# Moving the fourth group's convolution taps, y's statistics, a state carry and one factor operation in a fused Mamba and mixture-of-experts kernel

## The reference

```python
x = x + LN(mamba(LN(x)))
x = x + LN(moe(LN(x)))

# mamba, 512 inner channels, 16 states
x_in, z = split(x @ W_in)
u = silu(causal_conv(x_in, conv_w, 4 taps) + conv_b)
dt, B, C = split(u @ W_xproj)
delta = softplus(dt @ W_dt + b_dt)
h[t] = exp(delta[t] * A) * h[t-1] + delta[t] * u[t] * B[t]    # for each channel and state
y[t] = sum over the states of h[t] * C[t]
out = ((y + D_skip * u) * silu(z)) @ W_out

# moe: a shared MLP of width 256, and 8 experts of width 128, the best 2 of a softmax router
out = shared(x) + sum over e of coef[e] * (silu(x @ gate[e]) * (x @ up[e])) @ down[e]
```

## Time and profile before

| | |
|---|---|
| three runs, median (lowest to highest) | 2396.18 us (2395.93 to 2397.23) |
| the profiled execution's own time | 2396.12 us |
| its span, first to last instruction | 2394.3 us |
| mean granted TensorE clock | 0.932 |
| busy: TensorE, VectorE | 87%, 91% of the span |
| busy: ScalarE, GpSimd | 70%, 80% of the span |

### The profile page before, as it was taken

One profiled execution on the slowest core, in us unless ns is written; L12 is line 12 of the kernel. 1 busy time (PEld: TensorE's weight loads), 2 busy tenths in 40 slices (PEclk: granted clock), 3 DMA queues, 4 the chain that ended last, 5 costly groups with the idle time before them and its releaser, 6 DMA issues. The chain is left out here.

```text
span 2394.3 us, 30302 instructions
## 1 busy us (share of the span) xinstructions
PE 2081.6 (87%) x9216; PEld 1359.5 (57%) x9216; DVE 2189.5 (91%) x3112; ACT 1666.7 (70%) x2484; POOL 1908.7 (80%) x1566
## 2 busy tenths in 40 slices
PE   6668989899898989989898998989889898996977
PEld 2345565656556565665656556565655656565544
DVE  2999999999999999999999999999999999998950
ACT  4557777777877776877777687777777777775632
POOL 3576897969889797888979788797988979698844
PEclk8759999999999999999999999999999999998989
DMA  4111121111121111211111121121111211111201
GB/s 130 37 36 44 61 61 49 59 57 58 53 62 60 52 56 56 61 54 59 58 54 49 54 71 58 54 58 52 56 54 63 62 50 58 49 57 47 68 21 45
DMA packets 92946, 134.27 MB, mean 56 GB/s; under 512 B 12000, under 2 KB 42976, under 8 KB 92784
## 3 DMA queue, kind: packets, MB, share of 16 engines
q1 hardware_dynamic: 92784, 132.34, 18.3%
HBM read 123.13 MB, written 9.18 MB: 55 GB/s over the span
## 5 line engine op out<-in xcount | busy, mean ns | idle before, releaser
L793 DVE TENSOR_TENSOR_SCAN h<-d_a,carry,d_bu 128x512 f32<-128x512 f32 x1024 | 1262.1, 1267 | 53.6 <-ACT d_a L615 45.4
L1024 POOL TENSOR_TENSOR d_bu<-delta_u,b_rows 128x1024 f32<-128x1024 f32 x512 | 1202.2, 2362 | 4.9 <-DMA b_rows<-b_rows_hbm 0.8
L615 ACT ACTIVATE d_a<-delta,a_neg 128x512 f32<-128x512 f32 x1024 | 696.4, 689 | 481.7 <-DVE h L793 479.9
L449 PE MATMUL ht<-ident,h 128*128 128x128 f32 x4096 | 624.0, 299 | 148.0 <-DVE y_t L803 141.1
L449 PEld LDWEIGHTS ht<-ident,h 128*128 128x128 f32 x4096 | 515.4, 153 | 371.2 <-DVE y_t L803 142.1
L803 DVE SCALAR_TENSOR_TENSOR y_t<-ht,c_t,y_t 128x512 f32<-128x512 f32 x896 | 621.2, 735 | 2.7 <-PE ht L449 2.0
L524 PE MATMUL ring<-x_t,w_gate_sb 128*128 128x512 f32 x640 | 321.0, 627 | 23.1 <-ACT delta L758 19.0
L531 PE MATMUL ring<-x_t,w_up_sb 128*128 128x512 f32 x640 | 301.9, 616 | 22.7 <-ACT silu_gate L708 22.5
L551 PE MATMUL dn<-w_down_sb,up_hidden 128*128 128x256 f32 x1280 | 304.3, 381 | 15.8 <-POOL up_hidden L1082 15.8
L1077 POOL TENSOR_TENSOR up_hidden<-silu_gate,up_hidden 128x512 f32<-128x512 f32 x160 | 204.6, 1278 | 125.9 <-ACT up_hidden L712 77.4
L551 PEld LDWEIGHTS dn<-w_down_sb,up_hidden 128*128 128x128 f32 x1280 | 235.9, 190 | 77.4 <-issue 28.7
(11 more groups left out here) (114 smaller groups left out, 1922.0 us busy)
## 6 DMA issues: line engine op xcount, KB each, us to landing
b_rows<-b_rows_hbm SPq DMA_DIRECT2D x256, 256.0 KB, 3.5
coef_rows<-coef_rows_hbm SPq DMA_DIRECT2D x128, 256.0 KB, 3.4
xa<-L_attn_x_in SPq DMA_DIRECT2D x16, 512.0 KB, 5.0
xr<-L_attn_x_in SPq DMA_DIRECT2D x16, 512.0 KB, 5.2
out<-xr SPq DMA_DIRECT2D x16, 512.0 KB, 2.9
w_in_sb<-L_attn_W_in_in SPq DMA_DIRECT2D x1, 1024.0 KB, 6.3
w_gate_sb<-L_ffn_experts_gate_in SPq DMA_DIRECT2D x2, 512.0 KB, 4.9
w_up_sb<-L_ffn_experts_up_in SPq DMA_DIRECT2D x2, 512.0 KB, 5.6
```

The costliest lines, as they stand in the source:

```text
L449: last = nc.tensor.transpose(HT[q % HTS][:, j * P:(j + 1) * P], H[:, (NS * c + n) % HS, j, a * P:(a + 1) * P], IDN[:, :])
L615: nc.scalar.activation(DA[i % DAS][:, :], DL[:, r, j, :], ACT.Exp, scale=ANEG[:, j, n:n + 1]).then_inc(ex.sem, 1)
L793: nc.vector.tensor_tensor_scan(H[:, (NS * s + n) % HS, j, :], DA[(n * J + j) % DAS][:, :], BU[:, (2 * n + j // 2) % 4, j % 2, :], CARRY[:, ...
L1024: nc.gpsimd.tensor_tensor(BU[:, (2 * n + h) % 4, :, :], DU[:, 2 * h:2 * h + 2, :], BB[:, n % 2, :].unsqueeze(1).to_broadcast([P, 2, T]), A ...
```

## The change

Five things are moved or rewritten. The three taps of group 3 go from slot 11 to slot 12 on DVE, where they stand behind slot 12's scan and ahead of its two additions. The silu of u's groups 2 and 3 goes from slot 11 to slot 12 on ACT, and with it stands behind one more decay. y's statistics go from slot 60 to slot 61 on DVE. On POOL, the carry of state 15 goes behind the first inflow of slot 0. And y's factors take four operations in place of five: o's product is now negated when o's factors are made (four operations there in place of three), and y's last operation subtracts y's product from it.

```diff
-        shift = {w: stage(f"shift_{w}", n) for w, n in dict(xa=2, o=1, x1=2, y=3).items()}
+        shift = {w: stage(f"shift_{w}", n) for w, n in dict(xa=2, o=2, x1=2, y=2).items()}
...
-        XIN_PE, TAP0_ACT, CONV = (3, 4, 7, 8), (4, 5, 8, 8), (6, 7, 10, 11)
+        XIN_PE, TAP0_ACT, CONV = (3, 4, 7, 8), (4, 5, 8, 8), (6, 7, 10, 12)
...
-        Z_PE, Z_ACT, Y_STATS = 9, (8, 8, 9, 9), 60
+        Z_PE, Z_ACT, Y_STATS = 9, (8, 8, 9, 9), 61
         U_EARLY, HEAD_POOL = 7, 15
-        SILU = {11: [("u", 2), ("u", 3)], 60: [("z", j) for j in range(J)]}
-        SILU_FIRST = {11: SILU[11] + SILU[60]}
+        SILU = {12: [("u", 2), ("u", 3)], 60: [("z", j) for j in range(J)]}
+        SILU_FIRST = {12: SILU[12] + SILU[60]}
...
                 nc.gpsimd.tensor_tensor(MR[w][:, :], MV[w][:, :, 0], RS[w][:, :], ALU.mult)\
                   .then_inc(shift[w].sem, 1)
+                pool.wait_ge(shift[w].sem, shift[w].at(c, 1))
                 if w == "y":
-                    pool.wait_ge(shift["y"].sem, shift["y"].at(c, 1))
                     pool.wait_ge(shift["o"].sem, shift["o"].at(c))
-                    nc.gpsimd.tensor_tensor(MR["y"][:, :], MR["y"][:, :], MR["o"][:, :], ALU.add)\
+                    nc.gpsimd.tensor_tensor(MR["y"][:, :], MR["o"][:, :], MR["y"][:, :], ALU.subtract)\
                       .then_inc(shift["y"].sem, 1)
-                if w != "o":
-                    pool.wait_ge(shift[w].sem, shift[w].at(c, 2 if w == "y" else 1))
+                else:
                     nc.gpsimd.tensor_tensor(MR[w][:, :], MR[w][:, :], MINUS4[:, :], ALU.mult)\
                       .then_inc(shift[w].sem, 1)
...
                     if exists(lo - 2) and t == 0:
                         rstd_of("y", s - 2)
-                    if t == 0 and ffn:
-                        keep_state(s - 1, o, NS - 1)
...
                     if with_scan and n + 1 < NS and t % 2 == 0:
                         inflow(s, n + 1, t % NT // 2)
+                    if t == 0 and ffn:
+                        keep_state(s - 1, o, NS - 1)
```

## The result

The changed kernel takes 2381.6 us (median of 4 runs, 2381.41 to 2383.07), the kernel before 2396.05 us beside it: a ratio of 0.994, with a 95% interval from 0.9926 to 0.9953. The forecast was 2382.5 us, in a range of 2376 to 2389.

What follows compares the result with a forecast made beforehand. DVE, busy 91% of the span, was taken as the bound, with its work kept, so only its idle could go. Terms 5.6 + 5.9 + 0.4 + 0.3 + 1.4 = 13.6 us off 2396.12 gave 2382.5 us, range 2376 to 2389.

Steps and rivals of the forecast that it cites:

- Part A: Slots 11 to 14, taps and silu moved: 0.48 us gained a chunk, 1.1 lost in the first, 5.6 in all.
- the new wait of scan 12: Slot 11: without taps there, scan 12 waits 0.43 us for decay 12, against 0.91 gained at scan 14.
- ACT's room behind decay 16: ACT, slots 12 to 17: decay 16 can start at 1214.2, ACT is free at 1214.0, only 0.2 us of room.
- The slower rival: Slots 12 to 17: ACT's round ends too late if loads cost twice 1.28 us; 33 us lost, 2416; chance 0.03.
- Parts B and C: Chunk boundary: y's statistics moved and POOL's edits together gain 0.42 us at 14 boundaries, 5.9; neither does much alone.
- B: Slot 61: y's statistics no longer wait; scan 62 comes 0.50 us earlier, with 0.45 left at scan 63.
- The clock: TensorE's slow clock at chunk changes: 0.1 us a chunk credited, 1.4 in all; bounds 7.7 less, 5.4 more.
- the three lengths of before: Steady chunks of 140.54, 141.48 and 141.26 us, read as three reaches of TensorE's slow clock, 140.54 being clean.
- The ends: Last chunk ends 0.4 us earlier; one operation less in y's last factors behind it saves 0.3.
- Part C: POOL, into slot 4: scan 4 may start 0.43 us earlier, 0.28 for the operation and 0.15 for the carry.

Runs made afterwards that it cites:

- a_only: Kernel before, with only the taps of group 3 and the silu of u's last groups moved to slot 12; 2389.97 us, ratio 0.9972.
- silu_only: Kernel before, with the silu of u's last groups moved to slot 12 and the taps left in slot 11; 2404.63 us, ratio 1.0032.
- taps_only: Kernel before, with the taps of group 3 moved to slot 12 and the silu left in slot 11; 2398.35 us, ratio 1.0007.
- c_only: Kernel before, with only the carry put behind the inflow and four operations for y's factors on POOL; 2396.54 us, ratio 0.9999.
- warm: The change plus four matmuls a chunk, whose result nobody reads, on TensorE in slot 60; 2381.76 us, ratio 0.9932 to the kernel before.
- b_only: Kernel before, with only y's statistics moved to slot 61; 2389.78 us, ratio 0.9972.
- a_and_b: The change without the carry's move and with five operations for y's factors; 2383.04 us, ratio 0.9944 to the kernel before.
- decay_12_13: The change, with decay 12 ahead of z's last two copies and decay 13 ahead of x1's transposed copies on ACT; 2380.14 us, ratio 0.9931.
- pad_small: The change plus one idle DVE reduction of 128 x 192 values a chunk in slot 24; 2382.26 us, ratio 0.9937 to the kernel before.
- warm_12_13: decay_12_13 plus the four unread matmuls a chunk on TensorE in slot 60; 2379.71 us, ratio 0.9926 to the kernel before.

## Why the prediction was right

- **Part A**, forecast 14 x 0.48 - 1.1 = 5.6. Measured 0.45 a chunk in slots 11 to 13 of the change (7.79 for 8.24), and 1.4 lost in the first: 4.9. Scan 12 has its long wait there, 2.15 (the row below the list) for some 2.2 forecast. Both halves of the argument, the new wait of scan 12 and ACT's room behind decay 16, are shown by a_only, silu_only and taps_only. The slower rival had the right place (ACT's round too late for scans 15 and 17), but not the price of a table load: it comes true where the taps don't cover the round, in silu_only. Its price of a load came out nowhere: decay 16 of the change starts as its scan allows (the 0.26 above), and scans 15 and 17 wait for no decay.
- **Parts B and C**, forecast 0.42 x 14 = 5.9. Measured 0.34, 4.8, and all of it by B. The failed step is "Neither does much alone: without C, POOL holds scan 4 at 1181.02; without B, TensorE holds y_d at 1183.75". The second half is right (c_only). The first is true of scan 4 and wrong of the chunk: I stopped at the scan, and did not follow POOL's wait on to y_d, which then needed none. The term itself was also too large, in part because scan 2's wait grew by 0.10 (0.50 for 0.40), and only 0.06 was allowed for.
- **The clock**, forecast 1.4. The undisturbed chunk of the change is 140.54 - 0.46 - 0.34 = 139.74, as the runs with parts have it (139.70 in warm). The mean is 139.98, so the clock costs 0.24 for 0.52 before: 14 x 0.28 = 3.9. The credit was mis-sized by 2.5, within its bounds. Its reason was TensorE's shorter wait ahead of the slow stretch. That wait did get shorter (4.04 to 3.51), but b_only, which has it too, still pays 0.36 a chunk (140.56 for 140.20), hardly less than a_only without it (0.38). What gave the 0.28 is the common pace, and no line of the forecast had one: it drew among the three lengths of before.
- **The ends**, forecast 0.4 for the last chunk and 0.3 for the operation saved behind it. The last chunk gave 0.85. The operation is worth its 0.3, as the rows below the list show: from the start of y's last factors to the end of the span it is 9.87 before (2394.33 - 2384.46) and 9.58 after (2381.29 - 2371.71), and so it is in all 14 traces, 9.85 to 9.87 with five operations and 9.56 to 9.59 with four. But ahead of it, from the last scan to those factors, 1.3 is lost (91.45 and 92.76), and 0.6 before the first chunk. Neither is the change's doing as far as the runs show: from the last scan to the factors it is 91.45 to 93.04 in the 14 traces, and 92.67 in a_only, which leaves that work as it was; the first chunk starts at 55.32 to 57.03. Why they vary stays open.

The start of y's last factors, in POOL's timeline before and after:

```profile
2384.46 0.20 POOL L990 TENSOR_TENSOR var_eps_y<-mean_var_y,eps 128x4 f32<-128x4 f32 x1 [4.00 <-DVE mean_var_y L820]
...
2371.71 0.20 POOL L990 TENSOR_TENSOR var_eps_y<-mean_var_y,eps 128x4 f32<-128x4 f32 x1 [4.00 <-DVE mean_var_y L820]
```

Scan 12 of the first chunk, in DVE's timeline of the changed kernel, with its wait of 2.15 for decay 12:

```profile
84.17 1.28 DVE L793 TENSOR_TENSOR_SCAN h<-d_a,carry,d_bu 128x512 f32<-128x512 f32 x1 [2.15 <-ACT d_a L615]
```

The errors are -0.7 for A, -1.1 for B and C, +2.5 for the clock and -1.4 for the ends (0.85 + 0.3 - 1.3 - 0.6 for 0.7). They nearly cancel: 13.6 forecast, 13.1 between the profiled executions, 14.5 between the medians. So the number was in part luck, nearer than the account deserved. Part C, two of the five edits, bought the 0.3 at the end and nothing measurable in the chunks, where the forecast made the 0.42 hang on it.

## What to carry to other kernels

When a wait is shortened, follow it to the next place where two chains meet; if both arrive together there, shortening one moves the wait and gives nothing, and the one that is upstream of both gives all. A table-switching round on an in-order engine needs a place where the other engine has work of its own, so move both together. And when all repetitions of a loop take the same time to a hundredth, ask what holds them: here a gain of 0.4 inside the loop then gave nothing there, and a loss of 0.24 cost next to nothing.

## What had not been expected of the hardware

The clock of TensorE and the loop settle into step. In the kernel before, three chunks repeat as a pattern (140.54, 141.48, 141.26). In the change, a_and_b, decay_12_13 and pad_small, whose DVE work and waits differ by up to some 0.6 us a chunk (0.38 less in decay_12_13, 0.24 more in pad_small), most chunks take 139.9 to 140.0. Within each kernel the slow stretch lies at the same place of these chunks, to 0.1 us, but the place is not the same in all four. In the change it reaches from 2.6 ahead of scan 0 to 4.3 behind it (the chunk at 1167.77). Windows of pad_small and of decay_12_13 around a chunk's start (scan 0 at 1168.22 and 1164.15):

```profile
1164.48:1171.30 6.82, 5.47 (x24) 4.64 (x25) 6.37 (x8) 4.71 (x8) 6.61 (x7) 0.50 0.00 0
...
1162.31:1169.13 6.82, 5.47 (x26) 4.97 (x26) 6.33 (x7) 4.80 (x8) 6.45 (x8) 0.50 0.10 17
```

So it reaches 3.1 behind scan 0 where DVE has more to do, and 5.0 where it waits less. Where a chunk would come early, the stretch lies further into it and y_d waits for TensorE (0.16 and 0.57 in the change, 0.54 and 0.75 in decay_12_13); that costs just what was gained. My explanation, argued from this and from warm, is that the clock changes only at instants of its own, which the kernel's work does not move. By the Trainium skill, TensorE: Matmul & The Clock Gate, Part 1: The HAM clock gate, what watches the engine's activity is free-running and isn't set back when a kernel starts; the traces agree in so far as four kernels share one pace. What activity brings the clock back was not measured.

The best kernel measured is warm_12_13 with 2379.71 us, but its interval overlaps that of the change (0.9912 to 0.9941, and 0.9926 to 0.9953), so it is not shown to be faster.
